# Local layers of a macaron block: weighted values behind the next tile's projection, output product ahead of the scores, floor of the norms on VectorE

## What is computed

```python
def _layer(x, wqkv, qs, ksc, wo, lg, lb, w1, b1, w2, b2):
    h = shift_token(x)                      # second half of the columns from the row before
    q, k, v = jnp.split(h @ wqkv, 3, axis=-1)        # 8 heads of 64
    q, k = l2norm(q) * qs, l2norm(k) * ksc
    q, k = rotary_xpos(q, k)
    o = local_attention(q, k, v)            # windows of 64 rows, each sees itself and the one before
    x = x + o @ wo
    h = shift_token(x)
    h = (h - mu) / jnp.sqrt(var + 1e-05) * lg + lb
    a, g = jnp.split(h @ w1 + b1, 2, axis=-1)        # 341 hidden columns each
    return x + (a * gelu(g)) @ w2 + b2

def l2norm(t):
    return t / jnp.clip(jnp.linalg.norm(t, axis=-1, keepdims=True), 1e-12)
```

## Time and profile before

| | us |
|---|---|
| median of three runs | 3728.84 |
| profiled execution, its own time | 3723.46 |
| its span, first to last instruction | 3721.7 |
| TensorE matmuls busy | 3207.6 (86%) |
| VectorE busy | 2102.9 (57%) |
| ScalarE busy | 2087.8 (56%) |
| GpSimd busy | 1727.1 (46%) |
| mean granted TensorE clock | 0.966 of 2.4 GHz |

### The profile page before, as it was taken

One profiled execution on the slowest core, in us unless ns is written; L12 is line 12 of the kernel. 1 busy time (PEld: TensorE's weight loads), 2 busy tenths in 40 slices (PEclk: granted clock), 3 DMA queues, 4 the chain that ended last, 5 costly groups with the idle time before them and its releaser, 6 DMA issues. The chain is left out here.

```text
span 3721.7 us, 77077 instructions
## 1 busy us (share of the span) xinstructions
PE 3207.6 (86%) x28486; PEld 2018.8 (54%) x28612; DVE 2102.9 (57%) x4204; ACT 2087.8 (56%) x3388; POOL 1727.1 (46%) x1348
## 2 busy tenths in 40 slices
PE   6599999858889888579999999999998588899885
PEld 4222222635566666346666666666665355666663
DVE  4200000468887777455555555555556688777773
ACT  2499999335555555345555555555554355555552
POOL 1100000168888888223333333333332688888882
PEclk9799999979999999889999999999999799999998
DMA  1122221021111111000000000000000211111111
GB/s 34 22 37 39 36 38 25 7 83 38 34 35 35 35 34 30 14 9 10 6 6 8 6 6 8 6 8 6 6 8 2 85 35 34 35 35 35 34 31 32
DMA packets 124408, 95.75 MB, mean 26 GB/s; under 512 B 80448, under 2 KB 100544, under 8 KB 123968
## 3 DMA queue, kind: packets, MB, share of 16 engines
q1 hardware_dynamic: 122784, 89.41, 11.0%
q10 hardware_dynamic: 1440, 3.80, 0.3%
HBM read 22.90 MB, written 2.10 MB: 7 GB/s over the span
## 5 line engine op out<-in xcount | busy, mean ns | idle before, releaser
L1703 POOL TENSOR_SCALAR e<-e,inv 128x768 f32<-128x768 f32 (+7 forms) x512 | 375.0, 745 | 845.2 <-DVE inv L1599 845.2
L1668 ACT ACTIVATE e<-e,nmax 128x768 f32<-128x768 f32 (+7 forms) x512 | 396.0, 774 | 434.4 <-DVE e L1594 431.2
L530 ACT ACTIVATE e<-slot 128x1024 f32<-128x1024 f32 x512 | 472.6, 1091 | 38.5 <-PE slot L466 38.5
L1594 DVE TENSOR_SCALAR_CACHE_REDUCE e<-slot 128x768 f32<-128x768 f32 (+7 forms) x512 | 375.7, 753 | 161.4 <-PE slot L1504 161.4
L1515 PE MATMUL slot<-ident,e 128*128 128x128 f32 x2304 | 354.7, 281 | 32.5 <-DVE eT L1587 28.2
L880 POOL TENSOR_TENSOR inv_norm<-floored,minus_half 128x16 f32<-128x16 f32 x128 | 374.1, 2923 | 10.7
L1498 PE MATMUL slot<-key,q 64*128 64x512 f32 (+3 forms) x1536 | 317.2, 517 | 38.2 <-DVE e L1594 37.0
L1117 ACT ACTIVATE probT<-slot 128x1024 f32<-128x1024 f32 x128 | 131.0, 1023 | 372.1 <-PE slot L973 372.1
L852 POOL TENSOR_TENSOR prob<-prob,inv_total 128x1024 f32<-128x1024 f32 x128 | 242.7, 1896 | 200.8 <-DVE inv_total L1209 200.8
L873 POOL TENSOR_TENSOR rot<-cosine,sine 128x1024 f32<-128x1024 f32 x128 | 302.0, 2360 | 53.0 <-DVE sine L1191 52.8
L1587 DVE COPY eT<-slot 128x512 f32<-128x512 f32 (+3 forms) x384 | 237.8, 619 | 149.7 <-PE slot L1515 149.7
(11 more groups left out here) (156 smaller groups left out, 6322.1 us busy)
## 6 DMA issues: line engine op xcount, KB each, us to landing
v_mix<-v SPq DMA_DIRECT2D x256, 128.0 KB, 2.3
w_qkv<-in_causal_w_dram SPq DMA_DIRECT2D x32, 192.0 KB
query<-q_hi SPq DMA_DIRECT2D x128, 32.0 KB
keys<-q_hi SPq DMA_DIRECT2D x128, 32.0 KB
query<-q_lo SPq DMA_DIRECT2D x128, 32.0 KB
keys<-q_lo SPq DMA_DIRECT2D x128, 32.0 KB
hs<-H SPq DMA_DIRECT2D x32, 128.0 KB
h1s<-H SPq DMA_DIRECT2D x32, 128.0 KB
```

The source lines that it names most:

```text
L530: act.activation(e[n % E_RING][:], c.slots[n % RING][:].rearrange(flat), ACT.Exp, scale=2 * SCALE).then_inc(e_ready, 1)
L1594: dve.tensor_scalar(e[n % RING][h][:, 0:cols], c.slots[h][:].rearrange(flat)[:, 0:cols], -1.0, None, ALU.mult, ALU.min, accum_out=nmax[:, ...
L1668: act.activation(part, part, ACT.Exp, bias=nmax[:, n, h:h + 1], scale=-1.0, accum_out=total[:, n, h:h + 1]).then_inc(e_ready, 1)
L1703: pool.tensor_scalar(part, part, inv[:, n, h:h + 1], 1.0, ALU.mult, ALU.mult).then_inc(scaled, 1)
```

## The change

Four things are moved or altered.

On TensorE, `weighted` takes the tile `out` (four behind) in place of `turned` (three behind): it stands behind the query/key product of the next position, and before it in r3. It now waits for the values of the tile before `own` to be copied out (`last`). `project` stands before `scores`, and `pt` behind `t1` and `t3`. The second up product waits for `turned_out` of its position.

On ScalarE, `attention_out` stands behind `squares` except in r3, and `turned_out` behind `columns` and `t3`.

The floor of the squared norms goes from GpSimd (`inverse_norms`) to VectorE (behind the sums of `rotate`, with a wait for them). `floored` gets two buffers.

`inv_norm` gets a buffer for each of the four tiles of a group.

```diff
--- before.py
+++ after.py
@@ -682,8 +682,8 @@
         sine = sb("sine", [P, 1024])
         rot = sb("rot", [P, G, 2 * HEADS, D])
         norm2 = sb("norm2", [P, 2, 2 * HEADS])
-        floored = sb("floored", [P, 2 * HEADS])
-        inv_norm = sb("inv_norm", [P, 2 * HEADS])
+        floored = sb("floored", [P, 2, 2 * HEADS])
+        inv_norm = sb("inv_norm", [P, G, 2 * HEADS])
         v = sb("v", [P, G, HEADS * D])
         v_mix = sb("v_mix", [P, G, HEADS * D])
         qT = sb("qT", [P, 2, PAIRS, P])
@@ -842,7 +842,7 @@
                     pool.wait_ge(inv_norm_ready, a.t + 1)
                     pool.wait_ge(rot_ready, a.t + 1)
                     rows = rot[:, a.j, :, :]
-                    pool.tensor_tensor(rows, rows, inv_norm[:].unsqueeze(2).broadcast_to([P, 2 * HEADS, D]), ALU.mult)\
+                    pool.tensor_tensor(rows, rows, inv_norm[:, a.j, :].unsqueeze(2).broadcast_to([P, 2 * HEADS, D]), ALU.mult)\
                         .then_inc(unit_ready, 1)
 
                 def scale(a):
@@ -873,11 +873,8 @@
                     pool.tensor_tensor(rot[:, a.j, :, :].rearrange(flat), cosine[:], sine[:], ALU.add).then_inc(rot_ready, 1)
 
                 def inverse_norms(a):
-                    pool.wait_ge(norm2_ready, a.t + 1)
-                    pool.sem_inc(floor_ready, 1)
-                    pool.tensor_scalar(floored[:], norm2[:, a.j % 2, :], 1e-24, None, ALU.max).then_inc(floor_ready, 1)
-                    pool.wait_ge(floor_ready, 2 * a.t + 2)
-                    pool.tensor_tensor(inv_norm[:], floored[:], minus_half[:].broadcast_to([P, 2 * HEADS]), ALU.pow)\
+                    pool.wait_ge(floor_ready, a.t + 1)
+                    pool.tensor_tensor(inv_norm[:, a.j, :], floored[:, a.j % 2, :], minus_half[:].broadcast_to([P, 2 * HEADS]), ALU.pow)\
                         .then_inc(inv_norm_ready, 1)
 
                 def ticks(step, depth):
@@ -973,13 +970,13 @@
                         m = pe.transpose(bank_pt[:, s // 4, (s % 4) * P:(s % 4 + 1) * P], prob[:, a.j % 2, s, :], c.ident[:])
                     m.then_inc(pt_ready, 1)
 
-                def weighted(a, own):
+                def weighted(a, last):
                     pe.wait_ge(probT_ready, a.t + 1)
                     pe.wait_ge(v_mixed[a.j], 32 * a.g + 32)
                     if a.j or known(a.g, 1):
                         pe.wait_ge(v_mixed[a.j - 1], 32 * a.g + 32) if a.j else pe.wait_ge(v_mixed[G - 1], 32 * a.g)
-                    if own:
-                        pe.wait_ge(v_out, own.t + 1)
+                    if last:
+                        pe.wait_ge(v_out, last.t + 1)
                     else:
                         pe.wait_ge(attnT_ready, a.t)
                     for p in range(PAIRS):
@@ -1010,11 +1007,13 @@
                         m = pe.transpose(bank_ty[:, j * P:(j + 1) * P], z[:, j, :], c.ident[:])
                     m.then_inc(t3_ready, 1)
 
-                def up(a, k, own=None):
+                def up(a, k, own=None, turned=None):
                     if k == 0:
                         pe.wait_ge(zT_ready, a.g + 1)
                         if own:
                             pe.wait_ge(turn_ready, 3 * own.t + 3)
+                    if turned:
+                        pe.wait_ge(probT_ready, turned.t + 1)
                     if k == 2:
                         pe.wait_ge(hid_ready, CH * a.g + 2)
                     for g in (1, 0):
@@ -1033,18 +1032,20 @@
                 def ticks(step, depth):
                     for r in range(G):
                         own, turned, out = tile(step, r, 0, depth), tile(step, r, PT, depth), tile(step, r, OT, depth)
-                        scored = tile(step, r, TQ, depth)
+                        scored, last = tile(step, r, TQ, depth), tile(step, r, 1, depth)
                         ffn, ending = group(step, FFN, depth), group(step, DOWN, depth)
+                        if r == 3 and out:
+                            weighted(out, last)
                         if own:
                             qk(own, ffn if r == 3 else None)
+                        if r < 3 and out:
+                            weighted(out, last)
                         if scored:
                             tq(scored)
                         if r == 3 and ffn:
                             up(ffn, 2)
                         if own:
                             values(own)
-                        if scored:
-                            scores(scored)
                         if out:
                             if r == 0 and own and known(step, 1):
                                 pe.wait_ge(hT_ready, own.g + 1)
@@ -1053,21 +1054,21 @@
                             if r == 3 and ffn:
                                 pe.wait_ge(zT_ready, ffn.g + 1)
                             project(out)
-                        if turned:
-                            pt(turned, ffn if r == 3 else None)
+                        if scored:
+                            scores(scored)
                         if r == 3 and (ahead := group(step, -1, depth)):
                             if out:
                                 pe.wait_ge(h1_ready, out.t + 1)
                             t1(ahead)
                         if r == 2 and ffn:
                             t3(ffn, out)
+                        if turned:
+                            pt(turned, ffn if r == 3 else None)
                         if r == 0 and ending:
                             down(ending, out)
-                        if turned:
-                            weighted(turned, own)
                         if r == 2 and ffn:
                             up(ffn, 0, own)
-                            up(ffn, 1)
+                            up(ffn, 1, turned=turned)
 
                 t1(group(0, 0, None))
                 pe.wait_ge(band_ready, 1)
@@ -1135,13 +1136,16 @@
                         ffn = group(step, FFN, depth)
                         scored = tile(step, r, TQ, depth)
                         own, turned = tile(step, r, 0, depth), tile(step, r, PT, depth)
+                        out = tile(step, r, OT, depth)
                         if r == 3 and ffn:
                             gates(ffn, 0)
                             gates(ffn, 1)
-                        if out := tile(step, r, OT, depth):
+                        if r == 3 and out:
                             attention_out(out)
                         if own:
                             squares(own)
+                        if r < 3 and out:
+                            attention_out(out)
                         if scored:
                             heads(scored)
                         if r == 3 and ffn:
@@ -1149,12 +1153,12 @@
                             act.preload_act_table(ACT.Exp)
                         if own:
                             values(own)
-                        if turned:
-                            turned_out(turned)
                         if r == 3 and (ahead := group(step, -1, depth)):
                             columns(ahead)
                         if r == 2 and ffn:
                             t3(ffn)
+                        if turned:
+                            turned_out(turned)
                         if scored:
                             exp(scored)
                         if r == 2 and ffn:
@@ -1193,6 +1197,8 @@
                         dve.wait_ge(inv_norm_ready, a.t - 1)
                     dve.tensor_reduce(norm2[:, a.j % 2, :], sq[:].rearrange("p (h d) -> p h d", d=D), AX.X, ALU.add)\
                        .then_inc(norm2_ready, 1)
+                    dve.wait_ge(norm2_ready, a.t + 1)
+                    dve.tensor_scalar(floored[:, a.j % 2, :], norm2[:, a.j % 2, :], 1e-24, None, ALU.max).then_inc(floor_ready, 1)
 
                 def tops(a):
                     scores = bank_qs[:].rearrange("p a (h k) -> p (a h) k", k=P)
```

## The result

| | before | after |
|---|---|---|
| median (range), us | 3727.18 (3725.16 to 3732.86) | 3819.41 (3817.30 to 3825.61) |
| profiled execution: span, us | 3721.7 | 3823.8 |
| mean granted TensorE clock | 0.966 | 0.946 |
| VectorE busy, us | 2102.9 | 2214.9 |

A forecast was written before the change was run, and what follows sets the result against it. TensorE, GpSimd and VectorE were all taken as close to the bound. Step changes summed to 29.8 us a call, twice 59.6, on 3723.5 us, with 5.4 us to the median: 3788 us, range 3715 to 3840.

The forecast's parts named there:

- The hold: On VectorE, the moved floor was taken to wait until GpSimd's running tensor_tensor ends, at most 2.36 us.
- Rival A: The small tensor_scalar on VectorE is not held: 44.2 us for a straight step, 3679 us in all; chance 0.15.
- The places: Where the floor meets GpSimd in straight code: held behind the unit rows loses 0.5 us, through the rotated sum about 2.3.
- rival B: Floor held, but before the rotated sum almost everywhere outside the first layer's loop: 3761 us; chance 0.12.
- the walk: One step followed through all four engines: straight 47.4 us for 46.0, first layer's loop 54.4 for 48.5.
- rival C: TensorE pauses in the first layer's loop bring its clock down, 12 falls adding 48 us: 3836 us; chance 0.09.
- The main case: Floor on VectorE held behind GpSimd, 29.8 us more a call, 3788 us in all; chance 0.64 with Rival D.
- three steps of the first layer's loop: Per call, the floor is held behind the rotated sum in three positions of each step: 3 x 5.9 us longer.
- straight steps, with the last three positions: Per call, six steps of straight code, each longer by 1.5 us through the held floor.
- four steps of the second layer's loop: Per call, +1.9 us each, the middle between +3.0 held and +0.7 not held in r0.
- two early steps: Per call, steps taken as without feed-forward, positions falling from 9.88 to 9.1 us: -4.5 us together.
- Rival D: The values' wait for the attention copy costs what the weighted wait gave back; chance inside The main case's 0.64.

The follow-up runs named there:

- The first experiment: The changed kernel with the floor put back on GpSimd, all moves on TensorE and ScalarE kept: 3690.35 us, ratio 0.9896.
- the second: The kernel before the change with only the floor moved to VectorE, no order changed: 3838.76 us, ratio 1.0289.
- the third: The changed kernel with the floor at the same place on VectorE, done by a tensor_reduce in place of a tensor_scalar: 3705.32 us, ratio 0.9950.
- the filled kernel: The changed kernel with useless TensorE products in its pauses, ahead of t3 and of the first layer's down product: 3777.51 us, ratio 1.0130.
- The eleventh experiment: The changed kernel with the weighted product behind the query/key product in r3 of steps without a feed-forward: 3817.91 us, ratio 1.0232.
- The fillers: Useless TensorE products in pauses: in the changed kernel 3777.51 us, in the changed kernel with the floor back on GpSimd 3683.64 us.

## Why the prediction was right or wrong

**The hold: right, and shown.** That a 128x16 tensor_scalar is held like a 128x128 one was the step on which the sign hung. The first experiment puts 129 us on the floor in this order, the second 111 us on it in the old one, the third gives back 114 us with another instruction in the same place. Rival A fell: its 3679 us are what the kernel without a floor takes (3678), with a straight step of 44.4 us for A's 44.2. What A had wrong is the hold and the 15 us of an unheld floor; its walk of the rings was sound. The Trainium skill's rule ("SBUF — State Buffer", section "Who interferes with whom": whoever issues first has the pair and the other is fully blocked) agrees for the unit rows, the rotated sum and the addition, and not for the power, beside which a floor took 0.17 us. GpSimd's own instructions kept their lengths: unit rows 1.90 us on the mean before and 1.91 after, rotated sum 2.36 and 2.36.

**The places: right.** Forecast were a floor behind the unit rows in r0 and r2 and behind the rotated sum in r3 of straight code, and behind the rotated sum in r0, r2 and r3 of the first layer's loop. All came so (1.37, 1.37 and 1.30 us in the loop). The two timelines above show r2 and r3, and they were the reason against rival B. The timeline of VectorE in a straight step of the changed kernel has R, from r3 to the next r3, at

```profile
1114.20 0.20 DVE L1215 RECIPROCAL inv_total<-total 128x8 f32<-128x8 f32 x1
...
1126.41 0.20 DVE L1215 RECIPROCAL inv_total<-total 128x8 f32<-128x8 f32 x1
...
1137.12 0.20 DVE L1215 RECIPROCAL inv_total<-total 128x8 f32<-128x8 f32 x1
...
1148.16 0.20 DVE L1215 RECIPROCAL inv_total<-total 128x8 f32<-128x8 f32 x1
...
1162.34 0.20 DVE L1215 RECIPROCAL inv_total<-total 128x8 f32<-128x8 f32 x1
```

From R to R these are 12.2, 10.7, 11.0 and 14.2 us, for the 12.4, 10.65, 11.0 and 13.4 of the walk. Only r2 to r3 is off, by 0.8 us, and there the up products take 4.78 us at the lower clock, 1.08 more than in the filled kernel. Filled, it is 13.0 us and the step 46.97, where the walk had 47.4.

**The clock: the step that failed.** I gave rival C 0.09, on the ground that pauses of 1 to 1.5 us leave the clock at 1.00. But the holds of my own walk put t3 behind a late residual in straight steps as in the loop (3.12 us of pause measured there), and I weighed the rival by the pauses of the kernel before instead of by those of the walk. The main case put the clock at nothing. Measured in the first layer's loop: waits of 2.06 and 3.91 us, a clock of 0.91, from R to R 14.0, 15.6, 11.7 and 16.9 us for the 13.2, 13.7, 11.9 and 15.6 of the walk. Those furthest off are the two with the down product (4.54 us) and the up products (4.61) in them. Filled these two are 14.0 and 15.8, the step 54.5 to 55.6, against 54.4 of the walk. C's mechanism was there together with the main case. That its 48 us are near the 42 measured is luck: C put 4 us on each of twelve falls, all in the first layer's loop. A fall costs 1.7 us of the down product there and about 1 us of the up products, filling gives back 10 and 6 us in the loops of the two calls, and most of the rest comes back in straight code, where C had none. With C on top the forecast would have been 3836 us, 17 above the median measured.

**The call, term by term** (profiled executions, first call, start of the first query/key product to that of the last tile: 717.0 us before, 768.7 after, +51.7 for the 29.8 forecast; the first step, without a forecast, has 0.35 of them):

| term | forecast, us | measured, us |
|---|---|---|
| three steps of the first layer's loop | 17.7 | 28.8 |
| straight steps, with the last three positions | 9.0 | 15.5 |
| four steps of the second layer's loop | 7.6 | 2.9 |
| two early steps | -4.5 | +4.1 |

Of the first, the filled kernel has 18.7 us: what lies above the forecast is the clock's, but for 1 us. Of the second, 4.0 us lie in the last three positions, which I had counted as one more straight step of +1.5; the rest is within what filling gives back. The third: I took the middle between held (+3.0) and not held (+0.7) in r0. It is +0.75. The reason stands in the timelines of VectorE and GpSimd:

```profile
1369.69 1.21 DVE L1198 TENSOR_REDUCE norm<-sq 128x16 f32<-128x1024 f32 x1
```
```profile
1371.08 2.35 POOL L873 TENSOR_TENSOR rot<-cosine,sine 128x1024 f32<-128x1024 f32 x1
```

The squares' sum ends at 1370.90, just before the rotated sum starts, so the floor is held by the rest of the unit rows alone. The address work lies 0.37 us behind the reciprocal there, not the 0.59 of r1 that I had taken for r0. The fourth has the wrong sign, for two reasons. I priced the weighted product's move with the other positions, where it goes behind the query/key product; in r3 it goes ahead of it, and without a feed-forward nothing covers the copy of the transposes. Timeline of TensorE there:

```profile
839.60 0.34 PE L985 MATMUL slot<-probT,v_mix 128*64 128x64 f32 x4 [1.11 <-ACT probT L1118]
```

This is the 1.11 us of the earlier trace rows, which the change was to remove. The eleventh experiment puts the product back and the step is 2.4 us shorter. With it there, the first early step is 1.0 us shorter than before the change and not 1.4 us longer (four positions of 9.1 us would make it 3.1 shorter). The second early step, 2.7 us longer, I had read wrongly: it has a feed-forward, and its r2 is that of a straight step, held floor, late residual and slow products behind the pause included:

```profile
881.01 1.11 PE L1007 MATMUL slot<-ident,z 128*128 128x128 f32 x4 [3.32 <-DVE H L1220]
```

From r2 to r3 this step takes 19.4 us for 13.9 before; its first two positions gain 2.3 us.

**Rival D: small.** The values wait for the attention copy 0.24 us in a straight step of the first experiment, within the 0 to 0.6 us given, but 0.80 us in the early steps and 1.33 us in the first layer's loop of the changed kernel. The order as a whole gains 37 us.

**What stays open.** The 114 us between the held and the unheld floor are blocked time and the clock that falls behind it. The fillers give back 42 us of the changed kernel and 7 of the order alone; that makes some 35 us the clock's and some 80 the blocked time's, a difference of differences, and the first layer's loop stands at 0.96 even when filled. Why the clock falls in the second layer's loop in one call of the eleventh experiment and not in the other isn't known.

## What to carry to other kernels

Before a small tensor_scalar from SBUF to SBUF goes to VectorE, read in the timeline what GpSimd runs at that moment: behind a large tensor_tensor it costs the rest of that instruction, and everything that queues behind it on VectorE. Make it a reduction, or put it behind the instructions that others wait for, or where GpSimd is idle or in a power. Price a pause on TensorE by the clock behind it as well, and by the pauses of the new schedule, not of the old one.

## What the runs showed of the hardware that I had not expected

- Length is no matter to the hold: a 128x16 tensor_scalar takes 0.17 us beside a power instruction and up to 2.37 us beside a rotated sum. Of GpSimd's tensor_tensor that met a tensor_scalar here, only the power does not hold it, though it reads and writes SBUF too. Its rows are short as well (128x16 and 128x4); whether the operation or the short row makes the difference no run here tells.
- The clock does not follow the length of one pause. With the same 3.12 us ahead of t3 the straight step stands at 0.96 and its up products take 4.78 us; in the second layer's loop they take 3.69 us:

```profile
1394.40 0.65 PE L1007 MATMUL slot<-ident,z 128*128 128x128 f32 x4 [3.12 <-DVE H L1220]
...
1396.00 3.69 PE L1020 MATMUL slot<-zT,w 128*128 128x512 f32 x8
```

  With the probability transposes first, the same 2.03 us of pause is followed by up products of 5.70 us in one step and of 3.70 us in another of the same kernel. What decides between them no run here shows.
- Products that serve nothing shorten a kernel by 42, 30 and 7 us where they keep the clock at its upper level.
